# Four layers of graph work on 2048 nodes: the neighbour sums of the first two layers by Strassen's seven products instead of eight

## The chip, the core and the metric

The kernel runs on one core of one Trainium2 chip. The metric is the device time of a whole execution in microseconds (us); lower is better. Three executions of the kernel before are shown, and one execution was taken by the profiler. Engines: PE is TensorE, DVE is VectorE, ACT is ScalarE, POOL is GpSimd, SP issues most DMAs.

## What is computed

The reference works on x of 2048 nodes by 512 features and on 67584 edges. Four blocks follow each other, each with a layer norm and a relu ahead of it and a residual after it: an attention with an edge bias, a GCN of three layers, a GCN of one layer with relu, and a graph layer with weighted edges. The part that matters here is the GCN of three layers:

```python
def _gcn_layer(x, row, col, norm, W, b, n):
    h = x @ W
    msg = h[row] * norm[:, None]
    out = jax.ops.segment_sum(msg, col, num_segments=n)
    return out + b
h = relu(_gcn_layer(x, row, col, norm, W1, b1, n))
h = relu(_gcn_layer(h, row, col, norm, W2, b2, n))
h = _gcn_layer(h, row, col, norm, W3, b3, n)
```

With norm = dis[row] * dis[col], the segment sum is a product of a dense 2048 x 2048 matrix of edge counts with the scaled rows of h.

## The kernel before

An edge stage and the attention fill the first 530 us; they keep the count matrix in SBUF as `count` (f16, 16 tiles of 128 source nodes, 4 column groups of 512 targets). Then `layers_pe`, `layers_act`, `layers_dve`, `layers_pool` and `layers_sp` write the programs of the five engines for `for layer in range(4): products(layer); sums(layer)` and a last stage. Each engine runs its own list in order; only semaphores couple them. The layers are numbered 0 to 3 here: 0, 1 and 2 are the GCN of three layers, 3 is the next block.

**products(layer)** makes h @ W for 16 node tiles of 128. Each tile takes 12 matmuls (L2239, 128 x 512 moving): values are carried as an f16 high part and an f16 low part, and the product as high*high, high*low and low*high. ACT makes the high part of a tile's input (`split_hi`, L2017 or L2019), DVE the low part (`split_lo`, L2457 or L2459) into two slots of `h_parts`. The result comes out of PSUM twice: ACT writes the high half of `g` (`product_hi`, L2042), DVE the low half (`product_lo`, L2520). Layers 1 and 2 have three PSUM banks for results (5, 6, 7), layer 0 two. In layer 0 DVE also adds the self loops to `count` (`add_loop`, L2526), and ACT and PE turn further tiles of x in (`relu`, `copy_turned`, L1988, L1996, L2183).

**sums(layer)** is the neighbour sum: for each of 4 target groups and 4 blocks of 128 it runs 16 source tiles x 2 parts = 32 matmuls (L2305) into banks 0 to 3, so 512 matmuls per layer. In layers 0 and 1 `g` is the stationary operand and `count` the moving one, so the result stands transposed, with the 512 columns of a group in the order (v g) of `count` and not in the order of the nodes. `finish` on DVE multiplies it by `dis_row` and writes `h_t` through a view at a stride of 64 elements (L2563), ACT adds bias and relu (`L2110`), DVE takes the largest value (`chunk_max`, L2482), and `h_scale` turns the largest value of each group into a power of two, with two small matmuls of PE in between (`peak_row` L2189, `peak_all` L2196). DVE also takes row sums and row maxima of `count` for later layers (`sum_out`, L2604 and L2605). In layer 2 `count` is stationary; DVE adds into `tiles` (L2571), takes the mean and variance (L2578, L2579), and after four blocks makes the norm (L2597 to L2600), which releases ACT's `relu` (L1988), which releases PE's `turn` (L2183) of the next block: in `between`, one group later, after source step 20 of 64.

Of the kernel before, what the change touches and what calls it, by code (L numbers as in the profile page):

```python
# [13 lines left out]
P = 128  # L14
# [1766 lines left out]
G_SHIFT = (2.0 ** -19, 2.0 ** -24, 2.0 ** -24, 2.0 ** -20, 2.0 ** -19)  # L1781
# [16 lines left out]
def layers_memory(nc, keep, m):
# [21 lines left out]
    m.stats = place("stats2", [P, 8 * PER], F32, AT_REST + 26880)  # L1820
    m.moments = m.stats[:, 6 * PER:].rearrange("p (t two) -> p t two", two=2)
# [11 lines left out]
def layers_smalls(mem, nc, m):  # L1833
# [8 lines left out]
    m.h_max = sb("h_max", [P, KT], F32)  # L1842
# [10 lines left out]

def raw_place(m, n):
# [6 lines left out]
              "relued_y yfin peak peak_row peak_one peak_all w_scaled h_scaled g_scaled b_scaled e_scaled odis1u odis2 unscaled y_scaled var_last std_last normed_last "  # L1861
# [11 lines left out]
def layers_sp(nc, io, keep, m, s, attended):  # L1873
# [46 lines left out]
    sp.wait_ge(s["agg"], 4 * NT)  # L1920
# [17 lines left out]

def layers_pool(nc, m, s, attended):
# [10 lines left out]
                       pattern=[[-GPC, GROUPS], [0, P // GPC], [-1, GPC]], channel_multiplier=1).then_inc(s["paired"], 1)  # L1950
    pool.wait_ge(s["in_b"], 64)
# [6 lines left out]
def act_tools(nc, keep, m, s):  # L1958
# [852 lines left out]
```

## Time and profile before

| what | value |
|---|---|
| three executions, median | 1401.78 us (1399.90 to 1404.13) |
| profiled execution, span | 1400.5 us (no other time of this execution is given) |
| busy, share of the span | PE 97%, PEld 60%, DVE 63%, ACT 41%, POOL 6% |
| mean granted TensorE clock | 0.991 of full speed |
| chain that ended last | PE 83%, DVE 11%, ACT 2% |
| its largest lines | PE L2305 31%, L2239 13%, L2369 12% |

The span is cut into instructions per engine; a wait is the idle time of an engine ahead of an instruction, put down to the semaphore that came last. Matmuls overlap each other in the records: the mean of one (379 ns) is longer than the distance from one to the next, so the distance is read from a row that holds many.

### The profile page before, as it was taken

To read this page: it belongs to the slowest core of one execution; us is meant where nothing else is said; L and a number is where in the kernel's file an instruction comes from. 1 tells how busy PE (TensorE), PEld (TensorE's weight loads), DVE (VectorE), ACT (ScalarE), POOL (GpSimd) and SP (SyncE) were. 2 spreads that over 40 slices of the span, in tenths; PEclk is the share of its full clock that TensorE was granted. 3 is DMA by queue.
4 is the path that set the end of the run, shared out by engine and by line. 5 is a ranking of instruction groups with operands and counts; after the bars stand their busy time and mean duration, and the time that the engine had idled before them with its cause. 6 is when DMAs were issued, how large, how long until landed. Compare 5 with 4: busy or idle time off the path is not lost.

```text
span 1400.5 us, 26694 instructions
## 1 busy us (share of the span) xinstructions
PE 1363.9 (97%) x11285; PEld 843.1 (60%) x11285; DVE 886.7 (63%) x1381; ACT 568.6 (41%) x980; POOL 88.0 (6%) x86
## 2 busy tenths in 40 slices
PE   9889999989998999999999999999999999999998
PEld 8779898989996655544444444454444445344443
DVE  7998998999988886567555666542354223532323
ACT  2666566656554457411142113221253224422312
POOL 3120010101002110000001000011100000000000
PEclk9999999999999999999999999999999999999999
DMA  9634344335348723000002000022210222563201
GB/s 335 227 114 148 137 138 137 126 119 177 120 146 286 238 94 108 1 31 1 0 0 61 0 0 1 1 59 77 68 40 29 73 71 78 200 212 104 91 0 60
DMA packets 71333, 136.92 MB, mean 98 GB/s; under 512 B 11908, under 2 KB 24324, under 8 KB 69798
## 3 DMA queue, kind: packets, MB, share of 16 engines
q1 hardware_dynamic: 68542, 123.98, 26.8%
q0 software_dynamic: 1280, 5.77, 1.5%
q10 hardware_dynamic: 1384, 5.38, 1.1%
q8 instruction: 92, 1.51, 0.5%
q14 instruction: 35, 0.29, 0.1%
HBM read 81.79 MB, written 53.32 MB: 96 GB/s over the span
## 4 chain that ended last, share of the span: by engine, by line
PE 83%; DVE 11%; ACT 2%; issue 2%; DMA 1%; POOL 0%; ACTq 0%; SPq 0%; DVEq 0%; POOLq 0%
PE banks L2305 31%; PE banks L2239 13%; PE banks L2369 12%; PE banks L1255 6%; PE banks L1655 4%; DVE x_sb L894 3%; PE banks L1192 3%; PE banks L1209 2%; PE banks L1266 2%; PE banks L1166 2%; DVE x_sb L877 1%; PE banks L2183 1%; PE banks L1625 1%; PE banks L298 1%; PE banks L1643 1%
## 5 line engine op out<-in xcount | busy, mean ns | idle before, releaser
L2305 PE MATMUL banks<-g,count 128*128 128x512 f16 x1024 | 227.6, 379 | 0.5 <-DVE tiles L2571 0.5
L2305 PE MATMUL banks<-count,g 128*128 128x512 f16 x1024 | 223.6, 379 | 0.0
L2239 PE MATMUL banks<-w_parts,h_parts 128*128 128x512 f16 x960 | 215.3, 379 | 1.7 <-DVE g L2520 1.4
L2305 PEld LDWEIGHTS banks<-count,g 128*128 128x128 f16 x1024 | 99.6, 98 | 118.0
L2305 PEld LDWEIGHTS banks<-g,count 128*128 128x128 f16 x1024 | 99.7, 98 | 113.6 <-DVE tiles L2571 1.0
L2369 PE MATMUL banks<-g,part 128*128 128x512 f16 x768 | 165.9, 379 | 0.0
L2239 PEld LDWEIGHTS banks<-w_parts,h_parts 128*128 128x128 f16 x960 | 91.2, 98 | 115.4 <-issue 11.4
L894 DVE TENSOR_TENSOR x_sb<-eb_parts,x_sb 128x4096 f16<-128x4096 f16 x64 | 146.0, 2281 | 0.0
L1255 PE MATMUL banks<-x_sb 128*128 128x128 f16 x2048 | 126.9, 221 | 11.9 <-DVE x_sb L894 11.8
L1255 PEld LDWEIGHTS banks<-x_sb 128*128 128x128 f16 x2048 | 120.9, 99 | 15.3 <-DVE x_sb L894 14.2
L2369 PEld LDWEIGHTS banks<-g,part 128*128 128x128 f16 x768 | 75.1, 98 | 90.6
L2652 DVE SCALAR_TENSOR_TENSOR part<-count,e_scale,part 128x1024 f16<-128x1024 f32 x29 | 37.2, 1284 | 105.9 <-ACT part L2136 105.9
L2110 ACT ACTIVATE h_gcn_t<-h_gcn_t,b_col,unscale 128x512 f32<-128x512 f32 x32 | 26.0, 813 | 169.2 <-DVE h_gcn_t L2563 169.2
L2136 ACT ACTIVATE part<-count,e_scale 128x1024 f16<-128x1024 f32 x29 | 33.3, 1148 | 110.9 <-PE banks L2369 110.9
L877 DVE TENSOR_TENSOR x_sb<-iota_src,keys 128x2048 f16<-128x2048 f16 x64 | 77.7, 1215 | 0.0
L2459 DVE TENSOR_TENSOR h_parts<-h_gcn_t,h_parts 128x512 f16<-128x512 f32 x48 | 39.6, 829 | 48.6 <-ACT h_parts L2019 48.6
L1266 PE MATMUL banks<-x_sb 128*128 128x64 f16 x1024 | 65.1, 190 | 0.0
L1267 PE MATMUL banks<-x_sb 128*128 128x32 f16 x1024 | 64.2, 178 | 0.0
L2520 DVE SCALAR_TENSOR_TENSOR g<-banks,g_scale,g 128x512 f16<-128x512 f32 x64 | 47.6, 747 | 22.1 <-ACT g L2042 22.0
L1266 PEld LDWEIGHTS banks<-x_sb 128*128 128x128 f16 x1024 | 60.8, 97 | 0.5
L1655 PE MATMUL banks<-wo_sb,att_t 128*128 128x512 f32 x128 | 58.7, 602 | 0.4 <-ACT att_t L1563 0.4
L1267 PEld LDWEIGHTS banks<-x_sb 128*128 128x128 f16 x1024 | 59.0, 96 | 0.1
(346 smaller groups left out, 1902.5 us busy)
## 6 DMA issues: line engine op xcount, KB each, us to landing
weight_dram<-w_new SPq DMA_DIRECT2D x60, 256.0 KB, 2.6
count<-weight_dram SPq DMA_DIRECT2D x29, 512.0 KB, 7.1
qk_dram<-stage SPq DMA_DIRECT2D x64, 128.0 KB, 2.6
tiles<-x_dram SPq DMA_DIRECT2D x32, 256.0 KB, 3.5
x_dram<-tiles SPq DMA_DIRECT2D x32, 256.0 KB, 2.8
count<-in_x SPq DMA_DIRECT2D x4, 1024.0 KB, 12.8
h<-in_x SPq DMA_DIRECT2D x16, 256.0 KB, 4.3
h_dram<-h_t SPq DMA_DIRECT2D x8, 512.0 KB, 3.3
```

The lines of the kernel that those rows point to most:

```text
L877: dve.tensor_tensor(m.hot_src[:, z].rearrange("p g (c two) -> p g c two", two=2), keep.iota_src[:].rearrange("p (c two) -> p c two", two=2 ...
L894: dve.tensor_tensor(m.hot_eb[:, z].rearrange("p g (t c) -> p g t c", t=NT), values, tiles, ALU.mult).then_inc(s["hots"], 1)
L1192: mm = pe.matmul(out, m.h_slab[slab % 2][:, zh, k, tile * P:(tile + 1) * P], keep.wq[:, zw, k, c * SCOLS:(c + 1) * SCOLS], start=n == 0, s ...
L1255: mm = pe.matmul(m.bias_ps[:, 0:NT * H], m.hot_src[:, z, g], parts[:, part], start=g == part == 0, stop=g == BATCH - 1 and part == 1)
L1266: pe.matmul(m.cw_ps[:, g, 0:2 * CCOLS], m.hot_src[:, z, g], m.hot_cw[:, z, g, 0:2 * CCOLS], start=True, stop=False)
L1267: mm = pe.matmul(m.cw_ps[:, g, CCOLS:2 * CCOLS], m.hot_src[:, z, g], m.hot_cw[:, z, g, 2 * CCOLS:CW], start=False, stop=True)
L1655: mm = pe.matmul(m.wo_ps[:, t % 2], m.att_t[:, k, :], keep.wo[:, k, :], start=k == 0, stop=k == KT - 1)
L2239: mm = pe.matmul(out, m.h_parts[:, slot, zh, k], m.w_parts[:, zw, k], start=n == 0 and layer != 3, stop=n == len(passes) - 1)
L2305: mm = pe.matmul(m.agg_ps[:, b], lhs, rhs, start=i == 0 and z == 0, stop=i == NT - 1 and z == 1)
L2369: mm = pe.matmul(m.banks[:, b], m.part[:, n % 3, z, b * P:(b + 1) * P], m.g[:, q, gz], start=q == 0 and (z, gz) == (0, 0), stop=q == NT - ...
L2459: dve.tensor_tensor(out, source, hi, ALU.subtract).then_inc(s["lo"], 1)
L2520: dve.scalar_tensor_tensor(lo, result, scale, hi, ALU.mult, ALU.subtract).then_inc(s["glo"], 1)
```

## The change

Layers 0 and 1 get `paired_sums` in place of `sums`. The 4 target groups are worked in two pairs: h = 0 takes groups 0 and 2, h = 1 takes 1 and 3. For a pair the sum is a 2 x 2 block product (two halves of the features by two halves of the sources, two target groups), and it is made by seven block products of 32 matmuls each instead of eight: 448 matmuls a layer instead of 512. Part by part:

- ACT copies a product's result once, unsplit, to `h_t` as f32 (L2143); DVE's `product_lo` is gone in layers 0 and 1. From `h_t` ACT makes the high parts (`operand_hi`, a cast of 128 x 1024) and DVE the low parts (`operand_lo`, a subtraction of 128 x 1024) of 7 operands x 2 quarters. The operands are A11, A12, A22, and S1 to S4, which are sums and differences made on DVE in f32 (`combine`, 128 x 1024, 8 a layer). 10 of the 14 need results of tiles 8 to 15.
- The moving operands T1 to T4 are sums and differences of `count` groups, made on DVE in the tile `mix` (f16), 12 instructions a pair, each into the place that PE has just used.
- Results: steps 1, 2 and 4 are copied out of PSUM by ACT (`keep_single`), step 3 and 4 go on in the same banks; the rest is joined on DVE (`first_sum`, `join`), and POOL does two operations a pair. All read PSUM in the order of the nodes (a stride of 8 elements) and write SBUF contiguously. `dis_row` is now laid down in the order of the nodes.
- Scales are taken by pair, not by group: one pair of `peak_row`, `peak_all` fewer each for two groups in layers 0 and 1.
- The row sums of `count` move from DVE to ACT (`row_sum`, 128 x 1024 with an accumulated sum, 16 a layer); the row maxima move from `sums` of layers 0 and 1 to `finish` of layer 2 (`count_peak`, one per block). `edge_scale` moves from layer 2 to layer 3.
- Layers 1 and 2 have five PSUM banks for results of products (5, 6, 7, 0, 1), not three. Self loops are added in pairs, ahead of the eighth tile. Three loads move to a later place in SP's list.

```diff
+PAIRS = 2
+HT = NT // 2
+HIGHS_AFTER = {3: [("A11", 0)], 7: [("A11", 1)], 11: [("A22", 0), ("A12", 0)], 12: [("S1", 0), ("S3", 0)], 13: [("S2", 0)], 14: [("S4", 0)],
+               15: [("A22", 1), ("A12", 1), ("S1", 1), ("S3", 1), ("S2", 1), ("S4", 1)]}
...
-    return 3 if layer in (1, 2) else 2
+    return 5 if layer in (1, 2) else 2
...
+        if layer < 2:
+            act.activation(m.h_t[:, :, t * P:(t + 1) * P], prod_bank(m, layer, t).rearrange("p (k n) -> p k n", k=KT), ACT.Copy,
+                           scale=scale).then_inc(s["ghi"], 1)
+            for name, q in HIGHS_AFTER.get(t, ()):
+                operand_hi(layer, name, q)
+            return
...
+    def keep_single(layer, h, step, place):
+
+        first = 2 * (h if step == 1 else 1 - h)
+        act.wait_ge(s["agg"], step_mark(layer, h, step))
+        if h == 0:
+            act.wait_ge(s["glo"], GLO[layer] + 10)
+        act.copy(by_class(place), bank_pair(m, first)).then_inc(s["kept"], 1)
...
+            keep_single(layer, h, 1, nodes(m, h, 2))
+            keep_single(layer, h, 2, nodes(m, h + 2, 2))
+            for t in rows[0:2]:
+                row_sum(t)
+            keep_single(layer, h, 4, nodes(m, h + 2, 0))
...
+            act.wait_ge(s["fin"], 4 * number + 1)
+            relu_sums(layer, h, (0, 1))
+            for t in rows[2:4]:
+                row_sum(t)
+            if h == 1:
+                split_hi(layer + 1, 0)
+                split_hi(layer + 1, 1)
...
+            if layer == 1 and h == 0:
+                pe.wait_ge(s["ghi"], NT * layer + NT - 1)
+            if h == 1:
+                pe.wait_ge(s["joined"], 4 * (pair - 1) + 2)
+            step(1, one, "A11", lambda i: m.count[:, i, h], True)
+            if pair:
+                pe.wait_ge(s["joined"], 4 * pair)
+            step(2, other, "S1", lambda i: m.mix[:, i], True, mixed("T1", 2))
+            pe.wait_ge(s["kept"], 3 * pair + 1)
+            step(3, one, "A12", lambda i: m.count[:, HT + i, h], False)
+            pe.wait_ge(s["kept"], 3 * pair + 2)
+            step(4, other, "S4", lambda i: m.count[:, HT + i, 2 + h], False)
+            pe.wait_ge(s["fin"], 4 * pair + 1)
+            step(5, one, "S3", lambda i: m.mix[:, i], True, mixed("T3", 2))
+            pe.wait_ge(s["kept"], 3 * pair + 3)
+            step(6, other, "S2", lambda i: m.mix[:, i], True, mixed("T2", 4))
+            pe.wait_ge(s["joined"], 4 * pair + 1)
+            step(7, one, "A22", lambda i: m.mix[:, i], False, mixed("T4", 4))
...
+                first_sum(layer, h)
+                split_lo(layer + 1, 0)
+                split_lo(layer + 1, 1)
+            largest(0, nodes(m, h, 0), AX.XY, relu_mark(layer, h, "C11"))
+            for part in range(4):
+                mix_two(layer, h, part)
...
                 settle(dve.bn_stats(m.stats[:, 6 * b:6 * b + 6], m.tiles[:, b]))
+                if layer == 2:
+                    count_peak(t)
                 op = dve.bn_aggr(m.moments[:, b], m.stats[:, 6 * b:6 * b + 6])
```

Three places of the order. **First**, ACT at the end of the products of layer 1. Before (L2017 makes the high part of an input, L2042 takes a result out of PSUM):

```order
L2017 ACTIVATE h_parts<-h_gcn_t,h_scale 128x512
L2042 ACTIVATE g<-banks,g_scale 128x512
L2017 ACTIVATE h_parts<-h_gcn_t,h_scale 128x512
L2042 ACTIVATE g<-banks,g_scale 128x512 x3
L1972 ACTIVATE w_parts_60<-w_raw,w_scale 128x512 x4
L2110 ACTIVATE h_gcn_t<-h_gcn_t,b_col,unscale 128x512 x12
```

and now (L2120 makes the high part of an input, L2143 takes a result out, L2161 makes the high part of an operand; S_q_0_n is the high part of a combined operand of quarter q):

```order
L2120 ACTIVATE h_parts<-h_gcn_t,h_scale 128x512
L2143 ACTIVATE h_gcn_t<-banks,g_scale 128x4x128
L2161 CAST g<-h_gcn_t 128x4x256 x2
L2143 ACTIVATE h_gcn_t<-banks,g_scale 128x4x128
L2161 CAST S_0_0_80<-h_gcn_t 128x1024
L2161 CAST g<-h_gcn_t 128x4x256
L2143 ACTIVATE h_gcn_t<-banks,g_scale 128x4x128
L2161 CAST S_0_0_84<-h_gcn_t 128x1024
L2143 ACTIVATE h_gcn_t<-banks,g_scale 128x4x128
L2161 CAST S_0_0_88<-h_gcn_t 128x1024
L2143 ACTIVATE h_gcn_t<-banks,g_scale 128x4x128
L2161 CAST g<-h_gcn_t 128x4x256 x2
```

The last results of the products are now taken out between operand casts, and `keep_single` (L2206) and the row sums (L2212) follow.

**Second**, ACT and DVE in the second pair of a layer. ACT now, from step 4's copy on (L2218 is bias and relu):

```order
L2206 COPY h_gcn_t<-banks 128x2x512
L2218 ACTIVATE h_gcn_t<-h_gcn_t,b_col,unscale 128x512 x2
L2212 ACTIVATE banks,stats_78<-count 128x1024 x4
L2120 ACTIVATE h_parts<-h_gcn_t,h_scale 128x512 x2
L2218 ACTIVATE h_gcn_t<-h_gcn_t,b_col,unscale 128x512 x6
L2120 ACTIVATE h_parts<-h_gcn_t,h_scale 128x512 x3
```

DVE now, at the same place (L2885 is `first_sum`, L2685 a low part of the next layer's input, L2710 `largest`, L2807 `mix_two`, L2890 `join`, L2814 `mix_four`):

```order
L2885 TENSOR_TENSOR h_gcn_t<-banks,dis_row 128x2x512
L2685 SCALAR_TENSOR_TENSOR h_parts<-h_gcn_t,h_scale,h_parts 128x512 x2
L2710 TENSOR_REDUCE h_max<-h_gcn_t 128x1
L2807 TENSOR_TENSOR mix<-mix,count 128x1024 x4
L2890 TENSOR_TENSOR h_gcn_t<-banks,h_gcn_t 128x2x512
L2814 TENSOR_TENSOR mix<-count,mix 128x1024 x4
L2890 TENSOR_TENSOR h_gcn_t<-banks,h_gcn_t 128x2x512
L2926 TENSOR_TENSOR h_gcn_t<-h_gcn_t 128x2x512
```

None of it stands in the program before, where a group had L2563, L2110 and L2482 alone.

**Third**, DVE at one block of layer 2, before:

```order
L2571 SCALAR_TENSOR_TENSOR tiles<-banks,odis1u,tiles 128x512
L2578 BN_STATS stats_78<-tiles 128x6
L2579 BN_AGGR stats_78<-stats_78 128x2
L2597 TENSOR_SCALAR rstd<-stats_78 128x4
L2599 RECIPROCAL rstd<-rstd 128x4
L2600 SCALAR_TENSOR_TENSOR shift<-stats_78,rstd 128x4
```

and now, with `count_peak` (L2978) between the statistics and their aggregate:

```order
L2947 SCALAR_TENSOR_TENSOR tiles<-banks,odis1u,tiles 128x512
L2954 BN_STATS stats_78<-tiles 128x6
L2978 TENSOR_REDUCE count_max<-count 128x1
L2957 BN_AGGR stats_78<-stats_78 128x2
L2972 TENSOR_SCALAR rstd<-stats_78 128x4
L2974 RECIPROCAL rstd<-rstd 128x4
L2975 SCALAR_TENSOR_TENSOR shift<-stats_78,rstd 128x4
```

## Rows read from the trace of the kernel before

**Rows 1.** Windows of the layers; PE, PEld, DVE, ACT, POOL busy, clock, DMA share, GB/s.

```profile
585.00:697.00 112.00, 112.00 (x523) 50.96 (x522) 72.64 (x95) 16.38 (x22) 0.00 (x0) 1.00 0.03 10
697.00:740.00 43.00, 42.38 (x197) 18.95 (x196) 24.41 (x48) 19.75 (x30) 0.00 (x0) 1.00 0.00 1
740.00:852.00 112.00, 112.00 (x522) 50.93 (x521) 72.37 (x94) 16.66 (x22) 4.95 (x4) 1.00 0.06 19
896.00:1017.00 121.00, 120.45 (x598) 59.52 (x596) 40.98 (x92) 21.65 (x35) 15.10 (x12) 1.00 0.21 59
```

**Rows 2.** The chain that ended last, by engine.

```profile
PE 83%; DVE 11%; ACT 2%; issue 2%; DMA 1%; POOL 0%; ACTq 0%; SPq 0%; DVEq 0%; POOLq 0%
```

**Rows 3.** Timeline of PE: start us, us, engine, line, operands, count, idle before.

```profile
547.83 1.04 PE L2183 MATMUL banks<-ident,h_gcn 128*128 128x128 f32 x8
...
594.88 0.27 PE L2189 MATMUL banks<-ident,peak 128*1 128x128 f32 x1
594.99 2.32 PE L2305 MATMUL banks<-count,g 128*128 128x512 f16 x10
597.24 0.38 PE L2196 MATMUL banks<-line,ones 1*128 1x8 f32 x2
597.56 25.21 PE L2305 MATMUL banks<-count,g 128*128 128x512 f16 x116
...
740.01 10.52 PE L2305 MATMUL banks<-count,g 128*128 128x512 f16 x48
...
938.03 0.60 PE L2183 MATMUL banks<-ident,h_gcn 128*128 128x128 f32 x4
```

**Rows 4.** DVE instructions grouped by line and form: busy us, mean ns.

```profile
L877 DVE TENSOR_TENSOR x_sb<-iota_src,keys 128x2048 f16<-128x2048 f16 x64 | 77.7, 1215 | 0.0
L887 DVE TENSOR_TENSOR x_sb<-x_sb,w_parts 128x1024 f16<-128x1024 f16 x64 | 43.6, 682 | 0.0
L2605 DVE TENSOR_REDUCE count_max<-count 128x1 f32<-128x2048 f16 x16 | 36.4, 2276 | 0.0
L2563 DVE TENSOR_TENSOR h_gcn_t<-banks,dis_row 128x512 f32<-128x512 f32 x32 | 33.2, 1038 | 14.4 <-PE banks L2305 14.4
L1720 DVE TENSOR_TENSOR x_sb<-x_sb,banks 128x512 f32<-128x512 f32 x16 | 10.9, 680 | 0.0
L392 DVE TENSOR_TENSOR rec<-banks,be_row 128x512 f32<-128x512 f32 x8 | 5.5, 685 | 2.8 <-PE banks L298 2.5
L825 DVE TENSOR_TENSOR h_t<-h_first,h_t 128x1024 f16<-128x1024 f32 x1 | 1.2, 1220 | 0.0
```

**Rows 5.** ACT instructions grouped by line and form.

```profile
L2110 ACT ACTIVATE h_gcn_t<-h_gcn_t,b_col,unscale 128x512 f32<-128x512 f32 x32 | 26.0, 813 | 169.2 <-DVE h_gcn_t L2563 169.2
L1102 ACT CAST h_t<-h_first 128x1024 f16<-128x1024 f32 x1 | 1.0, 1037 | 0.0
L1044 ACT ACTIVATION_READ_ACCUMULATOR w_spare<-w_spare 128x1 f32 x4 | 0.8, 199 | 0.0
```

**Rows 6.** Timeline of ACT.

```profile
546.60 1.51 ACT L1988 ACTIVATE h_gcn<-x_sb,shift,rstd 128x512 f32<-128x512 f32 x2
...
735.09 0.72 ACT L2017 ACTIVATE h_parts<-h_gcn_t,h_scale 128x512 f16<-128x512 f32 x1 [1.29 <-PE banks L2239]
735.72 0.67 ACT L2042 ACTIVATE g<-banks,g_scale 128x512 f16<-128x512 f32 x1
...
935.60 1.52 ACT L1988 ACTIVATE h_gcn<-tiles,shift,rstd 128x512 f32<-128x512 f32 x2 [0.44 <-DVE shift L2600]
```

**Rows 7.** Timeline of DVE, first group of layer 2.

```profile
928.15 0.75 DVE L2571 SCALAR_TENSOR_TENSOR tiles<-banks,odis1u,tiles 128x512 f32<-128x512 f32 x1
...
935.40 0.16 DVE L2600 SCALAR_TENSOR_TENSOR shift<-stats,rstd 128x4 f32<-128x4 f32 x1
```

**Rows 8.** Windows of 3 us around a wait of PE early in the program.

```profile
39.00:42.00 3.00, 0.08 (x1) 0.08 (x2) 2.43 (x11) 1.52 (x2) 0.00 (x0) 0.88 0.61 218
42.00:45.00 3.00, 2.75 (x12) 2.36 (x13) 2.66 (x5) 1.54 (x3) 1.27 (x2) 0.50 0.03 8
45.00:48.00 3.00, 3.00 (x8) 2.26 (x8) 2.94 (x11) 1.53 (x2) 0.82 (x1) 0.50 0.76 195
48.00:51.00 3.00, 2.32 (x15) 1.90 (x14) 2.08 (x16) 1.72 (x5) 0.05 (x1) 0.98 0.40 81
```

More of the change, by code:

```diff
@@ L2147, in layers_act @@
         products(layer)
-        sums(layer)
+        if layer < 2:
+            paired_sums(layer)
+        else:
+            sums(layer)
     products(4)
@@ L2286, in sums, with beside @@
+    def beside(layer, h, number, i):
+        if (number, i) == ((3, 6) if h == 0 else (3, 2)):
+            peak_row()
+        if (number, i) == ((4, 4) if h == 0 else (4, 2)):
+            peak_all()
     def sums(layer):
@@ L2351, in layers_pe @@
         products(layer)
-        sums(layer)
+        if layer < 2:
+            paired_sums(layer)
+        else:
+            sums(layer)
     products(4)
@@ new lines, in await_used, with mix_two @@
+    def await_used(layer, h, step, part):
+        if part < 3:
+            dve.wait_ge(s["mix_used"], used_mark(layer, h, step, part))
+        else:
+            dve.wait_ge(s["agg"], step_mark(layer, h, step))
+    def mix_two(layer, h, part):
+        tiles = slice(2 * part, 2 * part + 2)
+        await_used(layer, h, 5, part)
+        dve.wait_ge(s["mixed"], mix_mark(layer, h, "T3", part // 2))
+        dve.tensor_tensor(m.mix[:, tiles], m.mix[:, tiles], m.count[:, tiles, h], ALU.add).then_inc(s["mixed"], 1)
@@ new lines, in mix_four, with operands @@
+    def mix_four(layer, h, part):
+        tiles = slice(2 * part, 2 * part + 2)
+        await_used(layer, h, 6, part)
+        dve.wait_ge(s["mixed"], mix_mark(layer, h, "T2", part))
+        dve.tensor_tensor(m.mix[:, tiles], m.count[:, HT + 2 * part:HT + 2 * part + 2, h], m.mix[:, tiles], ALU.subtract).then_inc(s["mixed"], 1)
+    def operands(layer, t):
+        if t == 3 or t == 7:
+            operand_lo(layer, "A11", t // 7)
+        if t == 11:
+            operand_lo(layer, "A22", 0)
+            combine(layer, "S1", 0)
+            operand_lo(layer, "A12", 0)
+            combine(layer, "S3", 0)
+        if t == 12:
+            operand_lo(layer, "S1", 0)
+            combine(layer, "S2", 0)
+        if t == 13:
+            operand_lo(layer, "S3", 0)
+            combine(layer, "S4", 0)
+        if t == 14:
+            operand_lo(layer, "S2", 0)
+            operand_lo(layer, "S4", 0)
@@ L2528, in products, with last_operands @@
+    def last_operands(layer):
+        operand_lo(layer, "A22", 1)
+        combine(layer, "S1", 1)
+        operand_lo(layer, "A12", 1)
+        combine(layer, "S3", 1)
+        operand_lo(layer, "S1", 1)
+        combine(layer, "S2", 1)
+        operand_lo(layer, "S3", 1)
+        combine(layer, "S4", 1)
+        operand_lo(layer, "S2", 1)
+        operand_lo(layer, "S4", 1)
     def products(layer):
@@ L2658, in layers_dve @@
         products(layer)
-        sums(layer)
+        if layer < 2:
+            paired_sums(layer)
+        else:
+            sums(layer)
     products(4)
```

401 lines of the change are left out of this document (298 added, 103 removed).

## Prediction

> **What bounds the kernel now.** I read the table of windows first, to see per layer which engine is full [rows 1]. In the neighbour sums of layers 0 and 1 PE is busy for 112.0 of 112 us, and in their products for 42.4 of 43. The chain that ended last says the same: 83% of it is PE [rows 2]. The clock stands at its full level, 2.4 GHz, in all these windows. So a matmul taken away is worth its whole distance, and a wait of PE that is put in costs its whole length. Nothing else counts: DVE has 72.6 of 112 us, ACT 16.4. The timeline of PE gives the distance: a row of 116 matmuls takes 25.21 us, of which 379 ns are the last one's own length, so (25.21 - 0.38)/115 = 0.216 us [rows 3]. A pair of `peak_row` and `peak_all` adds 0.11 + 0.32 = 0.43 us (594.88 to 594.99, 597.24 to 597.56) [rows 3].
>
> **What is removed.** 64 matmuls in each of two layers: 128 x 0.216 = 27.65 us. Two scale pairs fewer in each of two layers: 4 x 0.43 = 1.7. Together 29.35 us, all on PE. Layer 2 gives a pair to layer 3, which is zero. DVE's loss of `sum_out` (L2604, L2605) frees nothing that PE waits for.
>
> **Prices of the new work.** DVE, 128 x 1024 with an f32 source: 1.22 us by the one row of that shape (L825) [rows 4], 1.25 with the gap to the next one that waits for it; this holds for `operand_lo`, `combine`, `join`, `largest`. `mix` in f16: 1.22 for 2048 elements, 0.68 for 1024 (L877, L887) [rows 4]. ACT: a cast of 128 x 1024 1.04 (L1102), bias and relu 0.81, reading an accumulator 0.20 [rows 5], so a row sum is about 1.3. Nothing in this kernel shows POOL at 1024; it is off the path by my times up to 2 us of delay.
>
> The joins read PSUM at a stride of 32 bytes. The trace has that stride: L392 reads PSUM so and takes 685 ns for 512 elements, against 680 for the contiguous L1720, while L2563, which writes SBUF at a stride of 256 bytes, takes 1038 [rows 4]. So I price strided PSUM reads at nothing. The Trainium skill speaks against it: "SBUF — State Buffer", in its part on cachelines, gives SBUF lines of 16 bytes and PSUM lines of 8 and says that non-contiguous PSUM access significantly slows matmuls, in my words that a stride beyond a line is paid for on either side. L2563 agrees for SBUF, L392 does not for a DVE read of PSUM; the row decides.
>
> **Waits that come in, one by one**, found by walking the in-order lists of PE, ACT and DVE with these prices.
>
> Layer 0, products, 5.3 us. (a) The self loops of tiles 0 and 1 now stand ahead of the first low part: 0.55. (b) After result 3, ACT casts A11 (1.04) before the two relus whose turn was already due: the relus end at 548.1 and the turn began at 547.83 [rows 3, 6], so about 0.9 of it shows; after result 7, and by the strided write of `dis_row`, 0.3. (c) From result 11 on, DVE stands in low A22, S1, low A12, S3 (4 x 1.25) before it reaches the low part of input 14. Counted from the end of product 11: A22 cast by 2.5, four steps 7.5, low part 8.2; product 14 was due at 5.2, so 3.05. The next low part comes behind two more steps: 0.5.
>
> Layer 0, first pair, 1.5 us. Step 3 needs ACT's copy of step 1, which stands behind the last of six operand casts. That cast waits for eight DVE steps (10 us) after A22's: done 13.9 us after the products' end, copy 15.0, while two steps of 32 x 0.216 = 6.91 end at 13.8: 1.15. `mix_two` behind ACT's four weight parts and two relus: 0.35.
>
> Second pair, both layers, 2 x 5.0 us. After step 4 ACT does, in order, the copy (1.1), two relus (1.6), four row sums (5.2), two high parts (1.4): 9.2. DVE stands in the second low part until 10.0, then `largest` 1.2, then the first `mix_two` 0.7: 11.9. Step 6 of PE was due after step 5, at 6.9. Nothing else is there for PE.
>
> Layer 1, products into sums, 6.65 us. Banks 0 and 1 now hold results 13 and 14, and step 1 waits until 14 is out. In the trace the input cast before (735.09) and the result copy (735.72, 0.67) [rows 6] fix ACT's start; the sums began at 740.01 [rows 3]. Now: result 11 copied 736.4, A22 cast 737.4, then six DVE steps (low A22, S1, low A12, S3, low S1, S2) to 744.85, S2 cast 746.0, result 14 copied 746.6. This was fully hidden before. Then step 3 waits as in layer 0: 1.65, and 0.35 more.
>
> Change of layer, twice 1.4 us. After the last join (1.5 us behind PE) DVE takes four maxima and their maximum, 3.8 us, before the low part of input 2: 6.0 against 4.75, when PE asks. The scale chain then costs 0.75. The trace before has 0.6 there.
>
> Layer 2, 7.25 us. `count_peak` adds 2.28 - 0.08 = 2.20 per block (L2605 [rows 4]), four of them 8.8 between 928.15 and the norm's end at 935.56 [rows 7]. ACT's relu ended at 936.4 (935.60 [rows 6], first half of two) and PE's turn took it at 938.03 [rows 3]: 1.6 of slack. So PE waits 7.25. DVE's start at 928.15 stays, since it hangs on PE's own place. In later groups the norm has 9.1 us and needs 6. At the entry of layer 3, 0.85.
>
> Sum of the waits: 5.3 + 1.5 + 10.0 + 6.65 + 2.0 + 2.8 + 7.25 + 0.85 = 36.35. Against 29.35 that is +7.0.
>
> **The clock.** PE has no long wait in these layers now. Early in the program it was busy for 0.08 us of a 3 us window, and then the granted clock was 0.50, the 1.2 GHz level, for two windows of 3 us, and 0.98 in the third [rows 8]: 3.0 us lost, if the work is dense. The least is nothing. The two longest waits, 6.65 and 7.25 us, exceed that window well, and I charge 3.0 each. The first is followed by the wait of 1.65, which swallows as much: 4.35. The two waits of 5.0 us I leave to the range. "TensorE: Matmul & The Clock Gate" of the Trainium skill, on the clock gate, says too that the clock is halved after idleness; by it all four may fall.
>
> **Sum:** 1400.5 - 29.35 + 36.35 + 4.35 = 1411.9, say **1412 us**. The span used is 1.3 us under the median of the three runs, 1401.78; I don't add it, it is within their scatter. What a measurement of this kernel can tell from no change is about 0.3%, 4.2 us, so the border of slower is 1406.
>
> **Rivals.**
> 1. No fall of the clock: 1400.5 + 7.0 = 1407.5. For it: only one row shows a fall. Against: the waits are longer than there. Chance 0.10.
> 2. Strided PSUM reads are paid like L2563's write, (1038 - 680) ns per 512. Then a copy or join of 1024 costs 0.7 more: 1.0 at each of two step 3, 1.0 at each of two step 6, 0.7 at each change of layer: 5.4, 1417. That is what the SBUF page of the Trainium skill would give. Against it L392. Chance 0.08.
> 3. Faster than before. The f32 work of DVE from SBUF alone runs at the rate of its f16 work: 0.7 us instead of 1.25. L825 is one single record, and its shape is not quite that of `combine`. Then product 14 (-3.55), both step 3 (-2.8), half of step 1's wait (-3.3) with its fall of the clock (-1.35), and 2.5 us of each step 6 (with the copies) go, and 2 at the changes of layer: 18 us, 1394. It decides from about 0.95 us on for no change, 0.75 for faster. Against: every f32 row of 512 stands at 0.68 to 0.75. Chance 0.15.
> 4. My waits are too long by a third, because hand-overs overlap more than a walk shows, and the clock stays: 36.35 x 0.67 = 24.3, 1395.5; by a sixth with one fall of the clock 1404. Taken together around 1401. Chance 0.15.
> 5. That the change doesn't drop the eighth product is excluded by the order of the matmuls.
>
> The forecast has 0.52. Slower: forecast, rival 2 and most of rival 1, 0.67. Within 0.3%: most of rival 4 and the rest of 1, 0.16. Faster: rival 3 and a rest, 0.17. The range goes from rival 3's time to the forecast with both 5.0 us waits followed by a fall (+6) and some of rival 2: 1394 to 1420. The forecast's own range is 1406 to 1418.
>
> **What would show it.** PE at `paired_sums` has 896 matmuls at 0.216 us. In its waits stand, each once: about 3 us before product 14 of layer 0, 6.6 before step 1 of layer 1 released by ACT's result copy, 5 before step 6 of the second pair in both layers released by DVE `mix`, 7 before the turn in group 1 of layer 2 released by ACT's relu. `join` of 1024 at 1.2 us; 1.9 would be rival 2; `combine` at 0.7 rival 3. The clock under 1.00 in a window behind the long waits. The prediction is wrong if PE's waits in these layers sum to under 29 us, or if the largest of them stand elsewhere.

## The result and the profile after

| what | before | after |
|---|---|---|
| median of 4 runs each, same chip | 1402.65 us (1399.90 to 1404.13) | 1419.07 us (1417.60 to 1420.09) |
| ratio after / before | | 1.0121, 95% interval 1.0104 to 1.0137 |
| profiled execution | span 1400.5 us | 1420.09 us, span 1418.7 us |
| mean granted clock | 0.991 | 0.981 |
| first product of layer 0 to first product of layer 3 | 484.4 us (532.79 to 1017.18) | 503.1 us (531.20 to 1034.27) |

The change makes the kernel slower by 1.2%. The last line is the fairer measure of two profiles: the stages ahead of layer 0 end anywhere between 530.2 and 534.9 us in the profiled executions of this study, whatever the kernel. Inside that stretch the change costs 18.7 us.

The windows of the layers after, as in [rows 1]:

```profile
585.00:697.00 112.00, 107.68 (x490) 48.08 (x489) 72.56 (x86) 46.93 (x68) 13.23 (x4) 0.98 0.03 10
693.00:748.00 55.00, 44.76 (x199) 19.35 (x198) 34.06 (x52) 30.33 (x42) 2.33 (x1) 0.95 0.00 1
748.00:854.00 106.00, 101.86 (x454) 45.16 (x455) 66.79 (x81) 42.96 (x63) 11.30 (x4) 0.96 0.03 11
904.00:1034.00 130.00, 122.59 (x596) 60.27 (x593) 72.23 (x99) 21.90 (x35) 15.10 (x12) 0.97 0.20 55
```

PE was full or nearly so in these layers before; now it is idle for 4.3, 10.2, 4.1 and 7.4 us of them, and the granted clock, 1.00 before, is under it. DVE and ACT are far from full, so the order of their lists is the suspect; b1 below tests it. The chain by engine, as in [rows 2], has lost PE's share to DVE and ACT:

```profile
PE 76%; DVE 16%; issue 4%; ACT 4%; DMA 0%; DVEq 0%; ACTq 0%
```

PE's waits in sum (for whom; us in total, times, longest), without those of the stages before layer 0:

```profile
PE banks L2475 <- DVE mix L2807: 8.1, 2, 4.1
PE banks L2410 <- DVE h_parts L2685: 7.8, 4, 4.2
PE banks L2348 <- ACT h_gcn L2091: 7.5, 2, 6.9
PE banks L2475 <- ACT h_gcn_t L2143: 6.6, 1, 6.6
PE banks L2410 <- DVE h_parts L2687: 3.6, 2, 3.0
```

And where they stand, in the timeline of PE, as in [rows 3]:

```profile
582.52 6.92 PE L2410 MATMUL banks<-w_parts,h_parts 128*128 128x512 f16 x24 [3.01 <-DVE h_parts L2687]
589.27 7.07 PE L2475 MATMUL banks<-count,g 128*128 128x512 f16 x32
...
678.02 8.67 PE L2475 MATMUL banks<-mix,S 128*128 128x512 f16 x32 [4.07 <-DVE mix L2807]
686.53 7.07 PE L2475 MATMUL banks<-mix,g 128*128 128x512 f16 x32
...
701.56 3.80 PE L2410 MATMUL banks<-w_parts,h_parts 128*128 128x512 f16 x9 [3.21 <-DVE h_parts L2685]
...
747.91 9.56 PE L2475 MATMUL banks<-count,g 128*128 128x512 f16 x32 [6.57 <-ACT h_gcn_t L2143]
757.31 7.07 PE L2475 MATMUL banks<-mix,S 128*128 128x512 f16 x32
...
863.18 4.02 PE L2410 MATMUL banks<-w_parts,h_parts 128*128 128x512 f16 x9 [4.23 <-DVE h_parts L2685]
...
952.48 1.12 PE L2348 MATMUL banks<-ident,h_gcn 128*128 128x128 f32 x4 [6.91 <-ACT h_gcn L2091]
953.39 4.92 PE L2535 MATMUL banks<-g,count 128*128 128x512 f16 x12
958.15 0.60 PE L2348 MATMUL banks<-ident,h_gcn 128*128 128x128 f32 x4
```

Read each wait together with what follows it. An undisturbed step of 32 matmuls takes 6.91 us from start to start (589.27 to 596.18). Behind the wait of 4.07 us the same 32 take 8.51 us (678.02 to 686.53), behind 6.57 us 9.40. The windows of 3 us around the first of these show why: the clock (seventh number) is at its lower level behind the wait.

```profile
675.00:678.00 3.00, 0.00 (x0) 0.01 (x1) 3.00 (x5) 0.32 (x1) 0.00 (x0) 0.98 0.00 0
678.00:681.00 3.00, 2.98 (x8) 1.04 (x9) 2.82 (x4) 0.00 (x0) 0.00 (x0) 0.50 0.00 0
681.00:684.00 3.00, 3.00 (x15) 1.35 (x14) 1.39 (x2) 0.00 (x0) 0.00 (x0) 0.95 0.00 0
```

All seven waits of 3.0 us and more are followed by such a stretch. They cost 1.57 us (product 14), 1.60 and 1.42 (the two step 6), 2.49 (step 1 of layer 1), 1.70 and 2.81 (the changes of layer) and 2.64 (turn of layer 2), each as the distance of the rows less the same count at full clock; 0.49 more behind short waits in layer 0: 14.7 us. Only the fall behind product 14 is not certain: the same wait of 3.02 us is followed by none in the profiles of e4 and e5 below.

### The profile page after: what moved, and what is told of

Same layout as the page of the kernel before. It is cut to its first block, busy times and chain, and to the rows that moved or that the text cites. A ratio compares the mean times of both kernels' runs of the same rounds, so it can differ in the third digit from the quotient of the medians.

```text
span 1418.7 us, 26605 instructions
## 1 busy us (share of the span) xinstructions
PE 1346.3 (95%) x11145; PEld 828.2 (58%) x11145; DVE 928.6 (65%) x1374; ACT 643.6 (45%) x1084; POOL 114.1 (8%) x94
## 4 chain that ended last, share of the span: by engine, by line
PE 76%; DVE 16%; issue 4%; ACT 4%; DMA 0%; DVEq 0%; ACTq 0%
PE banks L2535 15%; PE banks L2410 12%; PE banks L2597 11%; PE banks L2475 11%; PE banks L1255 5%; PE banks L1659 3%; DVE x_sb L894 3%; PE banks L1192 3%; PE banks L1209 2%; PE banks L1266 2%; PE banks L1166 2%; DVE x_sb L877 1%; PE banks L2348 1%; PE banks L1629 1%; PE banks L1647 1%
## 5 line engine op out<-in xcount | busy, mean ns | idle before, releaser
L2410 PE MATMUL banks<-w_parts,h_parts 128*128 128x512 f16 x960 | 221.9, 387 | 12.0 <-DVE h_parts L2685 7.8
L1255 PEld LDWEIGHTS banks<-x_sb 128*128 128x128 f16 x2048 | 118.9, 98 | 16.4 <-DVE x_sb L894 15.3
L2475 PE MATMUL banks<-mix,S 128*128 128x512 f16 x256 | 59.6, 393 | 8.3 <-DVE mix L2807 8.1
L2475 PE MATMUL banks<-count,g 128*128 128x512 f16 x256 | 59.5, 391 | 6.8 <-ACT h_gcn_t L2143 6.6
L1266 PEld LDWEIGHTS banks<-x_sb 128*128 128x128 f16 x1024 | 60.3, 96 | 0.5
L2685 DVE SCALAR_TENSOR_TENSOR h_parts<-h_gcn_t,h_scale,h_parts 128x512 f16<-128x512 f32 x32 | 25.1, 789 | 52.2 <-ACT h_parts L2120 52.1
L1267 PEld LDWEIGHTS banks<-x_sb 128*128 128x128 f16 x1024 | 58.6, 96 | 0.1
L1006 ACT COPY bias<-banks 128x128 f32<-128x128 f32 x64 | 24.9, 389 | 70.1 <-PE banks L1255 70.0
```

The lines of the kernel that those rows point to most:

```text
L1255: mm = pe.matmul(m.bias_ps[:, 0:NT * H], m.hot_src[:, z, g], parts[:, part], start=g == part == 0, stop=g == BATCH - 1 and part == 1)
L1266: pe.matmul(m.cw_ps[:, g, 0:2 * CCOLS], m.hot_src[:, z, g], m.hot_cw[:, z, g, 0:2 * CCOLS], start=True, stop=False)
L1267: mm = pe.matmul(m.cw_ps[:, g, CCOLS:2 * CCOLS], m.hot_src[:, z, g], m.hot_cw[:, z, g, 2 * CCOLS:CW], start=False, stop=True)
L2410: mm = pe.matmul(out, m.h_parts[:, slot, zh, k], m.w_parts[:, zw, k], start=n == 0 and layer != 3, stop=n == len(passes) - 1)
L2475: mm = pe.matmul(m.agg_ps[:, bank + d], left, right(i), start=new and i == 0 and z == 0, stop=i == HT - 1 and z == 1, skip_group_check=not ...
```

## The experiments

Each kernel is the changed one with one edit, unless said otherwise. "Stretch" is the span from the first product of layer 0 to the first of layer 3 in the profiled execution: 484.4 us before, 503.1 after. In this one execution of the changed kernel POOL's additions of the bias row fell on DVE's low part at the second change of layer (1.77 us for it, 0.75 usual) and made that wait 4.23 us. Other profiled runs with the same code there have 3.35 to 3.8, so about 1.7 us of a difference to 503.1 (so much in e7) is not the edit's. The runs below went over three chips; each ratio is to the kernel before on the same chip, whose medians there were 1401.59 to 1402.22 us.

| run | median us | ratio to before, 95% | stretch us |
|---|---|---|---|
| changed kernel | 1419.07 | 1.0104 to 1.0137 | 503.1 |
| e1, high parts first | 1407.73 | 1.0023 to 1.0052 | 489.6 |
| e2, four maxima early | 1410.20 | 1.0037 to 1.0074 | 491.8 |
| e3, no POOL | 1417.57 | 1.0074 to 1.0139 | 497.4 |
| e4, SBUF strided | 1428.08 | 1.0154 to 1.0202 | 509.3 |
| e5, casts behind | 1419.13 | 1.0106 to 1.0140 | 499.6 |
| e7, filled wait | 1417.03 | 1.0088 to 1.0122 | 498.8 |
| b1, order | 1385.59 | 0.9860 to 0.9897 | 467.1 |
| b2, order, no POOL | 1377.98 | 0.9806 to 0.9838 | 460.0 |
| b3, as b2 with POOL | 1380.95 | 0.9826 to 0.9866 | 461.7 |
| b4, last moves | 1375.75 | 0.9803 to 0.9833 | 458.2 |

**e1, high parts first.**

```diff
             relu_sums(layer, h, (0, 1))
-            for t in rows[2:4]:
-                row_sum(t)
             if h == 1:
                 split_hi(layer + 1, 0)
                 split_hi(layer + 1, 1)
+            for t in rows[2:4]:
+                row_sum(t)
```

> Edit: in the second pair of both layers ACT makes the two high parts of the next layer's input ahead of its four row sums, not behind them. Theory A (step 6 of the second pair waits 4.07 us because DVE's low parts, largest value and mix stand in order behind ACT's row sums): the high parts end about 669.4, DVE's low parts 670.2, largest 671.4, first mix 672.1, and step 6 is due at 673.95, so both waits of 4.07 us go, and with them the slow clock behind each (1.60 and 1.42 us): 11.2 us less than the changed kernel's 1419.1, that is 1408. Rival B (DVE's own five steps are the limit, whichever order ACT has): half the wait stays, some 2 us at each, with a shorter slow stretch: 1412 to 1415. Rival C (the slow stretches have nothing to do with the waits): only the waits go, 8.1 us, 1411, and matmuls of step 6 still take 8.5 us for 32.

Measured 1407.7. Both waits of 4.07 us are gone, and step 6 takes its 6.91 us (676.82 to 683.73):

```profile
669.92 7.07 PE L2475 MATMUL banks<-mix,g 128*128 128x512 f16 x32
676.82 7.07 PE L2475 MATMUL banks<-mix,S 128*128 128x512 f16 x32
683.73 7.07 PE L2475 MATMUL banks<-mix,g 128*128 128x512 f16 x32
```

Theory A holds, to 0.3 us. PE waits for nothing that the row sums make, and these two calls in the wrong order cost 11 us.

**e2, four maxima early.**

```diff
-                if layer == 2:
+                if layer == 2 and c:
                     count_peak(t)
...
                 weight_spread(layer + 1)
+                count_peak(2 * layer)
+                count_peak(2 * layer + 1)
```

> Edit: the row maxima of the first four tiles (count_peak, 2.29 us each) leave the first group of layer 2; two are taken behind the first sum of the first pair of layer 0, two at the same place of layer 1, where DVE was idle for 7.5 us. The other twelve stay. Theory A (four maxima in front of the first norm make PE's wait of 6.91 us before the turn): the norm ends 8.8 us earlier, 1.9 us before PE asks, the wait of 6.91 goes and the slow clock behind it (0.47 in the turn, 2.17 in the twelve matmuls after) too: 9.5 us less than 1419.1, 1409.5. Rival B (the wait is POOL's addition or DMA of tiles, which comes late as well): the wait shrinks by less than 3 us, 1416 or more. Rival C: the maxima at their new place make steps 5 or 6 of the first pair wait, 2 us each layer, 1413.5.

Measured 1410.2: the wait of 6.91 us is gone (0.6 us of waits for ACT's relus remain, in layer 0) and no wait of step 5 or 6 of the first pair has come in. Theory A holds.

**e3, no POOL.** DVE does in `paired_sums` the two `tensor_tensor` that POOL had.

> Edit: the two operations of POOL per pair (add and multiply, 128x1024 f32) are done by DVE in the same place of its list; POOL has none. DVE then has 2 x 1.25 us more work per pair. Theory A (DVE and POOL hold each other up: DVE's multiply of 1024 takes 3.25 us and that of 512 2.14 us only because POOL works in SBUF at that time): both fall to 1.22 and 0.69, DVE's maxima at the change of layer begin about 0.7 us earlier than now, PE's waits there (3.21 and 4.23 us) fall to about 2.5 and 3.5 (the second still meets POOL's additions of the bias row), and the time is 1.5 to 3 us under 1419.1. Rival B (a multiply with a broadcast operand in place is slow in itself): 3.25 and 2.14 stay, a third such multiply adds 3.25 and an addition 1.25 a pair, and PE's waits at the changes of layer grow by 4.5 us each: 1428.

DVE's forms in the changed kernel (busy us, mean ns), as in [rows 4]:

```profile
L2774 DVE TENSOR_TENSOR h_gcn_t<-h_gcn_t 128x1024 f32<-128x1024 f32 x16 | 19.6, 1225 | 0.6
L2927 DVE TENSOR_TENSOR h_gcn_t<-h_gcn_t,dis_row 128x1024 f32<-128x1024 f32 x4 | 13.0, 3255 | 0.1
L2934 DVE TENSOR_TENSOR h_gcn_t<-h_gcn_t,dis_row 128x512 f32<-128x512 f32 x8 | 9.9, 1241 | 0.3
L2890 DVE TENSOR_TENSOR h_gcn_t<-banks,h_gcn_t 128x1024 f32<-128x1024 f32 x8 | 9.7, 1218 | 0.0
L2932 DVE TENSOR_TENSOR h_gcn_t<-banks,h_gcn_t 128x512 f32<-128x512 f32 x8 | 5.5, 681 | 1.2 <-PE banks L2475 1.2
L2885 DVE TENSOR_TENSOR h_gcn_t<-banks,dis_row 128x1024 f32<-128x1024 f32 x4 | 4.9, 1225 | 0.0
```

and the same two multiplies without POOL (L2920 and L2930 there):

```profile
L2930 DVE TENSOR_TENSOR h_gcn_t<-h_gcn_t,dis_row 128x512 f32<-128x512 f32 x8 | 5.5, 692 | 0.3
L2920 DVE TENSOR_TENSOR h_gcn_t<-h_gcn_t,dis_row 128x1024 f32<-128x1024 f32 x4 | 4.9, 1224 | 0.1
```

Theory A holds: 3255 becomes 1224 ns, 1241 becomes 692. The waits at the changes of layer are 2.13 and 2.61 us (+0.73 before the second scale matmul). The time is 1.5 us less, inside the forecast, but its interval overlaps that of the changed kernel, so the durations carry the verdict and not the time. Of the 5.7 us less in the stretch, the waits at the changes of layer are 2.2 (8.07 to 5.83 in sum, with those under 0.3); the rest is slow clock, which differs from profile to profile: behind the wait of 2.13 us it cost 1.70, behind that of 2.61 only 0.28. How the two engines hold each other up is to be seen in the changed kernel, DVE's timeline first, then POOL's:

```profile
688.59 1.23 DVE L2926 TENSOR_TENSOR h_gcn_t<-h_gcn_t 128x1024 f32<-128x1024 f32 x1
689.85 3.25 DVE L2927 TENSOR_TENSOR h_gcn_t<-h_gcn_t,dis_row 128x1024 f32<-128x1024 f32 x1
693.03 0.68 DVE L2932 TENSOR_TENSOR h_gcn_t<-banks,h_gcn_t 128x512 f32<-128x512 f32 x1
693.74 2.14 DVE L2934 TENSOR_TENSOR h_gcn_t<-h_gcn_t,dis_row 128x512 f32<-128x512 f32 x1
```

```profile
688.63 3.39 POOL L2051 TENSOR_TENSOR h_gcn_t<-h_gcn_t 128x1024 f32<-128x1024 f32 x1 [48.01 <-DVE h_gcn_t L2890]
692.10 3.23 POOL L2053 TENSOR_TENSOR h_gcn_t<-h_gcn_t,dis_row 128x1024 f32<-128x1024 f32 x1
```

DVE's first addition began 0.04 us ahead of POOL's and took its 1.23. DVE's multiply then ended 1.08 us after POOL's addition (692.02), about its own length (1.22 without POOL), which is what it would take if it did nothing until POOL was through. The join from PSUM at 693.03 took 0.68 with POOL at work. The multiply of 512 ended 0.55 us after POOL's end (695.33). The Trainium skill, "SBUF — State Buffer", section "SBUF: two separate sides", calls the port pair that DVE and GpSimd share an exclusive lock, which a DVE operation with two SBUF inputs needs against GpSimd. The trace agrees in all four of DVE's rows.

**e4, SBUF strided.** ACT's copies and DVE's sum and joins read PSUM contiguously and go to SBUF at a stride, as the kernel before did.

```diff
-    return values.rearrange("p d (g v) -> p d g v", g=GPC)
+    return values.rearrange("p d (g v) -> p d v g", g=GPC)
...
-    return m.banks[:, first:first + n].rearrange("p d (v g) -> p d g v", g=GPC)
+    return m.banks[:, first:first + n].rearrange("p d (v g) -> p d v g", g=GPC)
```

> Edit: the undoing of what the change's name says: ACT's copies and DVE's first sum and joins read PSUM contiguously and write (and read) SBUF at the stride of the classes, as the kernel before did; same values, same count of instructions. Theory A (the stride costs on SBUF's side alone, 1038 against 680 ns per 512 in the kernel before): joins and first sum of 1024 go from 1.22 to about 2.0 us, those of 512 from 0.68 to 1.04. On the path: one join of 1024 and two of 512 before each change of layer, 1.5 us each, so 3 us more, 1422. Rival B (neither side's stride costs in these forms): same durations, same time, 1419. Rival C (PSUM's stride does cost, and is hidden in today's 1.22): the joins get shorter than 1.22.

DVE's joins of 1024, 1218 ns in the changed kernel, and those of 512, 681 ns:

```profile
L2890 DVE TENSOR_TENSOR h_gcn_t<-banks,h_gcn_t 128x1024 f32<-128x1024 f32 x8 | 15.2, 1906 | 0.0
L2932 DVE TENSOR_TENSOR h_gcn_t<-banks,h_gcn_t 128x512 f32<-128x512 f32 x8 | 8.4, 1050 | 0.0
```

ACT's copies, 1012 ns in the changed kernel:

```profile
L2206 ACT COPY h_gcn_t<-banks 128x1024 f32<-128x1024 f32 x12 | 22.9, 1942 | 44.1 <-PE banks L2475 44.1
```

DVE's durations come out as theory A has them; read at a stride, PSUM is as fast as contiguously (681 ns for 512 against the 680 of L1720 [rows 4]). For ACT the nearest contiguous row is L1102, 1037 for 1024 against 1012 [rows 5], but that one reads SBUF. The time does not come out: 9.0 us more by the medians and 6.2 in the stretch, not 3. I had not priced ACT's copies (0.93 us each) and took what was hidden as hidden. Step 3 of the first pair now waits 1.60 and 1.14 us, step 6 of the first pair 0.86 in both layers, and the waits at step 6 of the second pairs and at the changes of layer grew by 0.6 to 1.1.

**e5, casts behind.** In layer 1 the casts of S1 to S4 of the first quarter stand behind result 15.

```diff
+HIGHS_LATE = {3: [("A11", 0)], 7: [("A11", 1)], 11: [("A22", 0), ("A12", 0)],
+              15: [("S1", 0), ("S3", 0), ("S2", 0), ("S4", 0), ("A22", 1), ("A12", 1), ("S1", 1), ("S3", 1), ("S2", 1), ("S4", 1)]}
```

> Edit: in the products of layer 1 alone ACT takes out results 12 to 15 first and makes the high parts of S1, S3, S2, S4 behind them; DVE's list is as it was. Theory A (step 1 waits for result 14, which stands behind casts that wait for DVE; but DVE's row of 1.25 us steps is the limit right behind it): step 1 starts at the end of the products, its wait falls from 6.57 to under 1 us, and step 2 then waits at its second half for the low part of S1 of the second quarter, which DVE has only some 10 us after step 1's old start: 5 to 6 us there. The time falls by at most 2 us, to 1417 to 1419. Rival B (only the two PSUM banks matter): the wait of 6.57 and the slow clock behind it (2.5) go, nothing comes in their place: 1410.

```profile
741.46 7.08 PE L2479 MATMUL banks<-count,g 128*128 128x512 f16 x32
748.38 3.62 PE L2479 MATMUL banks<-mix,S 128*128 128x512 f16 x16
757.67 6.30 PE L2479 MATMUL banks<-mix,S 128*128 128x512 f16 x16 [5.67 <-DVE S L2771]
```

Theory A holds: the wait of 6.57 us is 5.67 and stands a step and a half further on, with as much slow clock behind it (2.67 us against 2.49), and the time is the same, 1419.1. (The stretch is 3.5 us shorter; 1.7 of that is the scatter named above, and 0.7 that no slow clock followed product 14 here.) To free the bank alone gives next to nothing; DVE's row has to be put in the order of the due times as well.

**e7, filled wait.**

```diff
+            if layer == 2 and c == 1 and n == before[0]:
+                for k in range(24):
+                    pe.matmul(m.banks[:, 5], m.count[:, 0, 0, 0:P], m.g[:, 0, 0], start=True, stop=True)
```

> Edit: 24 matmuls that nobody reads (128x512, into a free PSUM bank, full speed 0.216 us each, 5.2 us together) stand ahead of the first turn of group 1 of layer 2, in front of which PE waited 6.91 us. Theory A (the slow stretch is what PE's own pause brings on, since the granted clock falls to 0.50 after it): the wait falls to 1.7 us, the turn comes at the same time, and what follows runs at the full clock: the twelve matmuls behind it take 2.59 us to the next turn, not 4.76, the four of the turn 0.44, not 0.91; the time falls by 2.6 us to 1416.5. Rival B (the slow stretch comes from something else at this place, the DMA traffic of the tiles or ACT and DVE at work): the twelve still take 4.7 us and the time stays at 1419.

```profile
954.55 0.66 PE L2348 MATMUL banks<-ident,h_gcn 128*128 128x128 f32 x4 [1.74 <-ACT h_gcn L2091]
955.05 2.75 PE L2535 MATMUL banks<-g,count 128*128 128x512 f16 x12
957.64 0.60 PE L2348 MATMUL banks<-ident,h_gcn 128*128 128x128 f32 x4
```

The turn comes as late as before, 16.15 us after the same place (938.40; in the changed kernel 936.33 to 952.48), but what follows runs at full clock: 3.09 us to the next turn, not 5.67. That is 2.58 us, as theory A has it. The median fell by 2.0, which alone would prove nothing, since the intervals overlap. But in the five profiles that have this wait unfilled (the changed kernel, e1, e3, e4, e5) the slow clock behind it cost 1.48 to 2.64 us, here under 0.1. So at this place the slow stretch comes from PE's pause, not from its neighbours.

**b1, order.** e1 and e2 with the operands in order of their due times (DVE's calls are moved to match, the weights' maximum is taken earlier, and ACT copies step 1 out between casts).

```diff
-LOW_ORDER = ("A11", 0), ("A11", 1), ("A22", 0), ("A12", 0), ("S1", 0), ("S3", 0), ("S2", 0), ("S4", 0), ("A22", 1), ("A12", 1), ("S1", 1), ("S3", 1), ("S2", 1), ("S4", 1)
+LOW_ORDER = ("A11", 0), ("A11", 1), ("A22", 0), ("S1", 0), ("A12", 0), ("A22", 1), ("S3", 0), ("S1", 1), ("A12", 1), ("S4", 0), ("S2", 0), ("S4", 1), ("S3", 1), ("S2", 1)
...
+HIGHS_AFTER = {3: [("A11", 0)], 7: [("A11", 1)], 11: [("A22", 0)], 12: [("A12", 0)], 13: [("S1", 0)],
+               15: [("A22", 1), ("S3", 0), ("A12", 1), ("S2", 0), ("S1", 1)]}
...
-        late = slots(layer) - 1
+        late = 2 if layer == 1 else slots(layer) - 1
```

> Edit: both moves of the first two runs (high parts ahead of row sums; four row maxima early) and a new order of the operands in both layers, made by due time: A22 and S1 of both quarters first, then what steps 3 to 5 need; A12 and S3 of a quarter no longer ahead of low parts of inputs; results of layer 1 are taken out two products late, not four; ACT copies step 1 out between casts, the weights' maximum is taken earlier. Theory A (every wait of PE in these layers is one of order, none of total work on DVE or ACT): product 14 of layer 0 (3.01 and 1.56 of slow clock) and step 1 of layer 1 (6.57 and 2.49) lose their waits as well, no wait over 1 us comes in before the change of layer, and the time is 1419.1 - 11.2 - 8.9 - 4.3 - 9.0 = 1385.7. Rival B (DVE is full there: 20 steps of 1.25 us from result 11 on): the waits move on to step 2 or 3 of the first pair, 4 us or more in each layer: 1394 or more.

Measured 1385.6, theory A. Neither product 14 nor any of the steps waits; a new wait of 1.63 us stands before input 4 of layer 1. The run changes all of this at once, so it shows that the waits were of order together, and not what each move gave.

**b2, order without POOL, and b3, the same with POOL.** Both make the parts of input 2 behind the first of the maxima.

```diff
         largest(1, nodes(m, h + 2, 0), AX.XY, relu_mark(before, h, "C12"))
+        if h == 1:
+            split_lo(layer, 2)
```

> Edit: as the run before, and at the change of layer the parts of input 2 are made between the maxima (behind the first of four), the two small matmuls of the scale come three matmuls later, and DVE does POOL's two operations. Theory A (the wait there is DVE's row of maxima ahead of the low part of input 2, made longer by POOL): the waits of 2.6 and 2.1 us (without POOL) fall under 1 us each, the slow stretches behind them go: against the run before 3.2 + 1.9 and 3.4 to 4.2 + 2 less, some 9 to 11 us: 1375 to 1377. Rival B (the maxima and the scale are the limit; what is gained before input 2 is lost before input 4): a wait of 2 to 3 us before input 4 in place of that before input 2: 1381 to 1384.

> Edit: as the run before (new order, parts of input 2 between the maxima), but POOL keeps its two operations per pair. Theory A (DVE and POOL hold each other up by 3.5 us at the change of layer, of which DVE doing POOL's work costs 2.5): DVE's multiply of 1024 takes 3.25 us again and the first of 512 about 2.1, DVE's maxima begin about 1 us later against PE's place than without POOL, PE's waits before inputs 2 to 4 grow by some 1 us in each layer: 1378 + 2 = 1380. Rival B (with the parts of input 2 early the joins' end doesn't matter any more): same time as without, 1378. Rival C (POOL's additions of the bias row, which come at the second change of layer, meet DVE's low parts too): as A and 1 us more in layer 2.

b2 is at 1378.0: between the theories. No wait before input 2 is left, but 2.27 us stand before input 4 of layer 1. ACT's list has a cause for it, which b4 tests: with two products' lateness the first two results stand ahead of the high part of input 4, and wait for `g_scale`. b3 is 3.0 us slower by the medians and 1.75 in the stretch, where 2 were forecast; the intervals overlap and the chips differ, and the verdict rests on the rows (3253 and 1240 ns again) and on PE's waits at the changes of layer, 6.5 us in sum against 4.7 in b2.

**b4, last moves.** Results 0 and 1 of layer 1 behind that high part, the maxima of the last two tiles out of group 3, self loops and A11's high parts one product later.

> Edit: the order without POOL's part, and four small moves: ACT takes out the first results of layer 1 behind the high part of input 4, not ahead of it; the maxima of the last two tiles go from group 3 of layer 2 to its start; self loops and the high parts of A11 come one product later; the two small matmuls of the scale one matmul later. Theory A (the last waits are each one of order): before input 4 of layer 1 2.27 us becomes 0.9 as in layer 2, at the entry of layer 3 1.09 goes, in layer 0 0.56 and 0.56 go: 1378.0 - 1.4 - 1.1 - 1.1 = 1374.4. Rival B (they are made by total work near them and come back one tile later): 1377 to 1378.

Measured 1375.75, against b2 2.2 us less where 3.6 were expected: the waits of 0.56 in layer 0 and 1.09 at the entry of layer 3 are gone, that before input 4 is 1.05, and waits of 0.83 to 0.99 at the changes of layer have come in beside it. So theory A holds in part: the intervals of b2 and b4 overlap, and some of what left one place came back at another, as rival B has it. The first line of b4's profile:

```profile
PE 1329.3 (97%) x11145; PEld 823.6 (60%) x11145; DVE 925.8 (67%) x1382; ACT 642.3 (47%) x1084; POOL 88.4 (6%) x86
```

Its stretch is 458.2 us; 484.4 less the 29.35 of the matmuls and scale pairs removed would be 455.0. So b4 beats both kernels: by 1.8% the one before, by 3% the changed one, with the same arithmetic (DVE does POOL's two operations a pair).

## Why the prediction was right, and where it was not

The forecast was 1412, slower; it came out slower at 1419.1, at the upper edge of the range of 1394 to 1420 and outside the forecast's own range of 1406 to 1418. The direction and the waits were earned; that the time still fell inside the range owes something to luck. The waits were put 2.8 us too high and the clock 10.4 too low, and the last 2 us of the range stood there for strided PSUM reads, which cost nothing. Term by term, in us:

| term | forecast | measured |
|---|---|---|
| matmuls and scale pairs removed | -29.35 | -29.35 (by the count; 32 matmuls still take 6.91) |
| waits, products of layer 0 | 5.3 | 3.9 (0.56 + 0.56 + 3.01 - 0.19 of before) |
| first pair of layer 0 | 1.5 | 0.2 |
| step 6 of the second pairs | 10.0 | 8.1 (twice 4.07) |
| layer 1, step 1 | 6.65 | 6.57 |
| layer 1, rest of the first pair | 2.0 | 0 |
| changes of layer, less those of before | 2.8 | 6.8 |
| turn of layer 2 | 7.25 | 6.91 |
| entry of layer 3 | 0.85 | 1.09 |
| sum of the waits | 36.35 | 33.6 |
| clock | 4.35 | 14.7 |

Span against span the change costs 18.2 us: 18.7 in the stretch, 1.1 behind it (the entry of layer 3), less 1.6 in the stages ahead, which scatter. The terms inside the stretch give 17.9; 0.8 us lies in hand-overs under 0.3 us.

- **The walk of the lists was right.** The five long waits that the prediction lists under "What would show it" came at their places, with the releasers named and within 1 us in length, and e1, e2, e5 and b1 show that their causes are those of the walk. Rival 4, waits too long by a third, falls: the sum was 8% less. The waits at step 3, forecast at 1.15 and 1.65 us, did not come: 0.18 and none. Slow clock ahead of them had made PE late already, which is a part of it: in e5, where layer 0 had no fall, 0.70 us stood there in place of 0.18. What took the rest was not looked for.
- **The step that failed is the clock.** "The two longest waits ... I charge 3.0 each" and "the two waits of 5.0 us I leave to the range" took the fall as likely for two waits. It came behind seven waits, those of 3.01 and 3.21 us among them, and cost 14.7 us, not 4.35. One fall was priced too high (1.4 to 2.8, not 3.0), their number too low by five. The length of the wait does not fix the price: behind the same wait of 6.57 us it was 2.49 here and 1.53 in e1. Rival 1, no fall, is refuted, and e7 shows the cause by itself. The Trainium skill, "TensorE: Matmul & The Clock Gate", section "Part 1: The HAM clock gate", has the clock halved after idleness; by it, the prediction said, all four of its longest waits may fall; it charged two. The trace agrees: 0.50 in the window behind the first wait of 4.07 us.
- **The second miss is the change of layer**: 2.8 against 6.8. "It is off the path by my times", said of POOL, left out that POOL holds DVE up. DVE's last multiplies took 2.0 and 1.45 us more, so in both layers the last one ended 3.7 us behind PE's last matmul, where the forecast had 1.5, and the maxima began late. Another 0.8 us is the one-off at the second change of layer (4.23 against 3.42 in e7). e3 shows the hold, but not what it is worth alone, because DVE took over POOL's 2.5 us a pair there.
- **Prices.** `join` 1218 ns, `combine` 1225, low part 1238: the forecast's 1.22 to 1.25; rival 3 falls. Strided PSUM reads cost nothing in these forms: rival 2 falls, as the row L392 had it. The Trainium skill, "SBUF — State Buffer", in its part on cachelines under "SBUF: two separate sides", has each access that crosses to a new line of SBUF pay a penalty. The trace agrees for SBUF (1.9 against 1.2 us in e4). Of PSUM the page speaks for matmuls alone, so the prediction stretched it when it took it for DVE's reads.

## What to carry to other kernels

When a change takes work from a full engine and gives order problems to its feeders, walk the in-order lists once for every new instruction and sort them by due time: here nearly the same instructions gave 1419 or 1376 us. Price a wait of TensorE with the slow clock behind it: waits of 3 to 7 us cost 1.4 to 2.8 us more here, and in e3 one of 2.13 us cost 1.7. Work that nobody waits for (row sums, maxima for later) belongs behind every instruction that someone does.

## What the hardware showed unexpectedly

- DVE and POOL exclude each other when DVE reads both operands from SBUF: 3255 against 1224 ns for 1024 f32 elements. A DVE operation with an operand in PSUM goes on (681 ns for 512 with POOL at work). Giving two operations to POOL was worth nothing here: DVE alone was 3.0 us faster in b2 against b3 by the medians (the intervals overlap), 1.75 us in the stretch.
- The stride was paid on SBUF's side by ACT too: 1942 against 1012 ns for a copy of 1024 out of PSUM.
- A pause of PE that was filled with matmuls nobody reads cost only its own length: 2.58 us came back in e7.
